# Self-attention value products in four row groups of 32 by 128 columns, their weights turned on VectorE, tokens laid in halves of four sequences

## What is computed

```
x = x + tanh(g_xattn) * xattn(layernorm(x), ctx)         # 16 heads of 128, 64 keys, q and k rms-normed
y = layernorm(x)
q, k, v = rmsnorm(y)*ln1 @ wq, wk, wv                    # self-attention, 16 heads of 128
attn = softmax(causal(q k^T / sqrt(128)))                # 64 x 64 for each sequence and head
y = y + (attn v) @ wo
t = rmsnorm(y)*ln2
routed = top-6 of 16 experts (176 units each), weighted; shared = one expert of 352 units
x = x + tanh(g_ffn) * (y + routed + shared)
```

## Time and profile before

| | |
|---|---|
| median of 3 runs | 628.91 us (628.39 to 629.61) |
| the profiled execution | 628.85 us |
| its span, first to last instruction | 627.1 us |
| PE, PEld | 619.1 us (99%), 541.5 us (86%) |
| DVE, ACT, POOL | 462.0 us (74%), 320.5 us (51%), 253.3 us (40%) |
| granted TensorE clock | 1.000 over the whole span |

### The profile page before, as it was taken

The page is one execution under the profiler, slowest core; times in us unless marked ns, Lnnn a source line. Parts: engine busy times, 40 slices in busy tenths (PEclk is TensorE's granted clock), DMA queues, the critical chain, the costliest instruction groups (busy, mean ns, idle before and its releaser), DMA issues.

```text
span 627.1 us, 18234 instructions
## 1 busy us (share of the span) xinstructions
PE 619.1 (99%) x7200; PEld 541.5 (86%) x7200; DVE 462.0 (74%) x930; ACT 320.5 (51%) x699; POOL 253.3 (40%) x336
## 2 busy tenths in 40 slices
PE   8999999999999999999999999999999999999997
PEld 6788888888889988999999889988888888888886
DVE  5979777997886886786677899565576987555556
ACT  6867677777743334242434333453477444444442
POOL 3221211313144334344343354345545665455453
PEclk9999999999999999999999999999999999999999
DMA  7532131111021322222231321123323233333332
GB/s 234 186 85 70 52 103 28 40 40 31 24 70 43 111 69 69 70 68 77 64 118 39 115 70 36 35 63 93 98 85 94 75 102 101 90 87 99 100 87 90
DMA packets 36023, 50.30 MB, mean 80 GB/s; under 512 B 4080, under 2 KB 23024, under 8 KB 35952
## 3 DMA queue, kind: packets, MB, share of 16 engines
q1 hardware_dynamic: 35376, 48.81, 26.2%
q10 hardware_dynamic: 576, 0.48, 0.2%
HBM read 48.22 MB, written 1.05 MB: 79 GB/s over the span
## 4 chain that ended last, share of the span: by engine, by line
PE 96%; DVE 1%; ACT 1%; DMA 1%; issue 1%; SPq 0%; DVEq 0%; ACTq 0%
PE acc L568 26%; PE bank_q L541 17%; PE bank_k L541 14%; PE bank_v L541 9%; PE bank_s L541 8%; PE bank_v L656 7%; PE bank_k L736 2%; PE bank_p L753 2%; PE bank_s L714 2%; PE bank_s L704 2%; PE bank_t L721 1%; PE bank_p L687 1%; PE bank_q L677 1%; PE bank_k L666 1%; DMA xt<-in_ctx_t 1%
## 5 line engine op out<-in xcount | busy, mean ns | idle before, releaser
L568 PE MATMUL acc<-wo_hi,pv_hi 128*128 128x256 f32 x328 | 93.4, 285 | 0.4 <-DVE pv_lo L1515 0.2
L568 PE MATMUL acc<-wo_lo,pv_hi 128*128 128x256 f32 x328 | 92.9, 283 | 0.0
L568 PE MATMUL acc<-wo_hi,pv_lo 128*128 128x256 f32 x328 | 92.0, 281 | 0.0
L1677 POOL TENSOR_TENSOR wq_lo<-raw_a,wq_hi 128x256 fp32r<-128x256 f32 x32 | 23.4, 732 | 116.9 <-DVE wq_hi L1452 116.9
L568 PEld LDWEIGHTS acc<-wo_hi,pv_hi 128*128 128x128 f32 x328 | 61.5, 188 | 5.3 <-issue 2.2
L1677 POOL TENSOR_TENSOR wq_lo<-raw_m,wq_hi 128x256 fp32r<-128x256 f32 x50 | 40.4, 808 | 59.8 <-DVE wq_hi L1471 58.3
L568 PEld LDWEIGHTS acc<-wo_lo,pv_hi 128*128 128x128 f32 x328 | 61.6, 188 | 2.2
L568 PEld LDWEIGHTS acc<-wo_hi,pv_lo 128*128 128x128 f32 x328 | 62.3, 190 | 0.0
L1515 DVE TENSOR_TENSOR pv_lo<-raw_a,pv_hi 128x512 fp32r<-128x512 f32 (+1 forms) x51 | 37.5, 737 | 31.8 <-ACT pv_hi L1104 31.5
L1104 ACT ACTIVATE pv_hi<-raw_a 128x512 fp32r<-128x512 f32 (+1 forms) x51 | 31.7, 623 | 56.1 <-DVE raw_a L1510 50.5
L541 PE MATMUL bank_q<-xt_hi,wq_hi 128*128 128x512 f32 x144 | 59.8, 415 | 0.0
(11 more groups left out here) (246 smaller groups left out, 1949.2 us busy)
## 6 DMA issues: line engine op xcount, KB each, us to landing
raw_m<-in_chunk_m SPq DMA_DIRECT2D x50, 256.0 KB, 2.8
raw_a<-in_head_a SPq DMA_DIRECT2D x48, 192.0 KB, 3.3
raw_b<-in_head_b SPq DMA_DIRECT2D x32, 256.0 KB, 3.0
raw_m<-in_chunk_m SPq DMA_DIRECT2D x50, 128.0 KB, 2.1
raw_v<-in_pair_v SPq DMA_DIRECT2D x16, 256.0 KB, 2.8
raw_b<-in_head_b SPq DMA_DIRECT2D x32, 128.0 KB, 2.1
xs<-in_x SPq DMA_DIRECT2D x6, 128.0 KB, 3.2
out<-xs SPq DMA_DIRECT2D x3, 256.0 KB, 2.5
```

Source lines behind the costliest of these rows:

```text
L568: last = nc.tensor.matmul(acc[t // 2][:, (t % 2) * D:(t % 2 + 1) * D], w[:, tok], m, start=begins and n == 0, stop=True, skip_group_check= ...
L1677: nc.gpsimd.tensor_tensor(lo, raw, hi, ALU.subtract).then_inc(signal, 1)
```

## The change

**Tokens.** The host lays `x` out so that a tile of 128 tokens holds one half (32 tokens) of each of four sequences. Tile `2n + part` has half `part` of sequences `4n` to `4n+3`. Before, it held two whole sequences. The output is laid back on the host. Access patterns change with it (`tokens_of`, `keys_of`, `queries_at`).

**Turning.** `turn_attn` on TensorE and `take_turned` on ScalarE go. `turn_weights` on VectorE (blocks of 32 by 32) now serves self-attention too.

**Value products.** They are formed in four row groups `j` of 32 rows by all 128 columns, each into its own bank, `bank_k`, `bank_v` (in the last pair `bank_q`), `bank_p`, `bank_t`. `k` runs over the two halves of the keys. For the first half (`k == 0`) both halves of the queries move (64 columns), for the second only the later one (32 columns), since the mask leaves the others at nothing. They leave PSUM in four steps instead of two.

**Around it.** `bank_k` and `bank_v` are now written by the value products, so the keys of the next pair's first head go to `bank_s`, and `head_values` waits until ScalarE has taken the values out of `bank_v`. Rounding `wo` moves from VectorE (`split_out`, L1485) to ScalarE (`round_out`). VectorE's `split_head_values` moves ahead of `subtract_max`. In cross-attention `place_variance` (L812, 8 small matmuls at the start of each half) goes, since the statistics now lie where they are added. In stage `m`, `bank_s` and `bank_k` change places.

```diff
         def turn_banks(u):
-            return (bank_t, bank_p) if u.kind == "a" else (bank_p, bank_s if u.kind == "b" else bank_t)
+            return (bank_t, bank_p) if u.kind == "a" else (bank_p, bank_t)
...
+        def head_bank(u, j):
+
+            return (bank_k, bank_v if u.deferred else bank_q, bank_p, bank_t)[j]
...
         def key_bank(u, h):
...
-            return (bank_s, bank_q)[h] if u.very_first else bank_k
+            return (bank_s, bank_q if u.very_first else bank_k)[h]
...
-            def turn_attn(u):
-                pe.wait_ge(B["norm"], u.n)
-                for b in range(G // 2):
-                    last = nc.tensor.transpose(bank_t[:, b * P:(b + 1) * P],
-                                               attn[:, 2 * b:2 * b + 2, :].rearrange("p t k -> p (t k)"), ident)
-                last.then_inc(B["t_done"], 1)
...
             def head_values(u):
 
                 pe.wait_ge(B["vs"], 2 * u.n)
                 pe.wait_ge(B["attn_t"], u.n)
-                turned = rows_t[:].rearrange("p n a q -> p (n a q)").rearrange("p (n a h q) -> p n h a q", a=2, h=2, q=GROUP)
+                if u.deferred:
+                    pe.wait_ge(B["vs"], 2 * u.n + 2)
+                else:
+                    pe.wait_ge(M["silu"], 1)
+                turned = rows_t[:].rearrange("p t h q -> p (t h q)")\
+                    .rearrange("p (a h n k q) -> p h n k a q", a=2, h=2, n=2, q=GROUP)
                 values = vs[u.n % 2]
-                for g in range(G):
-                    h, n = divmod(g, NT)
-                    cols = slice(g * SEQ, (g + 1) * SEQ)
-                    for c in range(P // SEQ):
-                        width = slice(h * P + c * SEQ, h * P + (c + 1) * SEQ)
-                        for r in range(SPB):
-                            rows = slice(r * SEQ, (r + 1) * SEQ)
-                            last = nc.tensor.matmul(value_bank(r)[c * SEQ:(c + 1) * SEQ, cols], values[rows, n, width],
-                                                    turned[rows, n, h], start=True, stop=True)
+                for h in range(2):
+                    for n in range(2):
+                        for k in range(2):
+                            for j in range(QUADS):
+                                rows = slice(j * GROUP, (j + 1) * GROUP)
+                                found = by_token(head_bank(u, j))[:, h, 2 * n + k:2 * n + 2]
+                                last = nc.tensor.matmul(found, values[rows, 2 * n + k, h * P:(h + 1) * P],
+                                                        turned[rows, h, n, k, k:], start=k == 0, stop=True,
+                                                        skip_group_check=True)
                 last.then_inc(B["pv_done"], 1)
...
             def take_head_values(u):
                 act_e.wait_ge(B["pv_done"], u.n)
-                for r in range(SPB):
-                    nc.scalar.activation(by_sequence(pv_hi[:], r), by_tile(value_bank(r)[:]), ACT.Copy).then_inc(B["pv_hi"], 1)
+                for j in range(QUADS):
+                    nc.scalar.activation(tokens_of(pv_hi[:], j), by_token(head_bank(u, j)), ACT.Copy).then_inc(B["pv_hi"], 1)
+
+            def round_out(u, h):
+                if u.n > 1:
+                    act_e.wait_ge(B["wo_done"], u.of(h) - 2)
+                act_e.wait_ge(ld_b2[h], 16 * u.n)
+                nc.scalar.activation(wo_hi[h][:], raw_b2[h][:], ACT.Copy).then_inc(B["wo_hi"], 1)
```

More of the change, by code:

```diff
@@ L413, in up_bank @@
         def up_bank(u):
-            return (bank_k, bank_s)[u.parity]
+            return (bank_s, bank_k)[u.parity]
         x_v = x.rearrange("(h t p) d -> h p t d", h=HALVES, p=P)
@@ L581, in output @@
                 else:
-                    pe.wait_ge(B["pv_lo"], u.of(1))
+                    pe.wait_ge(B["pv_lo"], QUADS * u.n)
                     pe.wait_ge(B["wo_lo"], u.of(h))
@@ L630, in project_keys @@
                 pe.wait_ge(stage["wk_lo"], u.of(h))
-                if h and bank is bank_k and u.kind == "b":
-                    pe.wait_ge(B["kt"], u.of(0))
+                if not h and u.kind == "b" and not u.very_first:
+                    pe.wait_ge(B["scaled"], u.n - 1)
                 if h and bank is bank_q:
@@ L702, in scores @@
                             at = (n * QUADS + j) * SEQ
-                            queries = slice(at + part * GROUP, at + (part + 1) * GROUP)
                             last = nc.tensor.matmul(bank_s[j * GROUP:(j + 1) * GROUP, g * SEQ:(g + 1) * SEQ],
-                                                    qt[:, h, queries], kt[:, h, at:at + SEQ], start=True, stop=True)
+                                                    qt[:, h, queries_at(n, part, j)], kt[:, h, at:at + SEQ], start=True, stop=True)
                     last.then_inc(A["scores"], 1)
@@ L711, in scores @@
                     for j in range(QUADS):
-                        at = (2 * j + n) * SEQ
-                        queries = slice(at + part * GROUP, at + (part + 1) * GROUP)
-                        last = nc.tensor.matmul(bank_s[j * GROUP:(j + 1) * GROUP, g * SEQ:g * SEQ + seen], qt[:, h, queries],
-                                                kt[:, h, at:at + seen], start=True, stop=True)
+                        keys = kt[:, h].rearrange("p (n a j c) -> p n j a c", a=2, j=QUADS, c=GROUP)[:, n, j, 0:part + 1]
+                        last = nc.tensor.matmul(bank_s[j * GROUP:(j + 1) * GROUP, g * SEQ:g * SEQ + seen],
+                                                qt[:, h, queries_at(n, part, j)], keys, start=True, stop=True)
                 last.then_inc(B["scores"], 1)
-            def turn_attn(u):
-                pe.wait_ge(B["norm"], u.n)
-                for b in range(G // 2):
-                    last = nc.tensor.transpose(bank_t[:, b * P:(b + 1) * P],
-                                               attn[:, 2 * b:2 * b + 2, :].rearrange("p t k -> p (t k)"), ident)
-                last.then_inc(B["t_done"], 1)
             def context_values(u):
@@ L767, in prepare @@
                 piece, step = piece_at(u)
-                if piece in ("turn", "logits", "spread") and u.kind == "b":
-                    pe.wait_ge(B["scaled"], u.n)
                 if piece == "turn":
@@ L803, in release @@
                     pe.wait_ge(semaphore, value)
-            def place_variance(u):
-                pe.wait_ge(eps_ready, u.half + 1)
-                variance = eps_var[:, u.half, :].rearrange("p (n t) -> p t n", n=2)
-                for j in range(QUADS):
-                    for part in range(2):
-                        row = j % 2 * SEQ + part * GROUP
-                        nc.tensor.matmul(bank_q[j * GROUP:(j + 1) * GROUP, HT // 2 + part * 2:HT // 2 + part * 2 + 2],
-                                         ident[:, row:row + GROUP], variance[:, j // 2], start=True, stop=True)
             def cross_pair(u):
@@ L869, in self_pair @@
                     project_gate(nxt)
+                    pe.wait_ge(B["scaled"], u.n)
                     project_up(nxt)
-                    pe.wait_ge(B["pv_lo"], prev.of(1))
+                    pe.wait_ge(B["pv_lo"], QUADS * prev.n)
                     prepare(u)
@@ L876, in self_pair @@
                     held = prepare(u)
-                turn_attn(u)
                 if nxt.kind == "b":
@@ L893, in chunk @@
                 if u.very_first:
+                    pe.wait_ge(B["pv_lo"], QUADS * (prev.n - 1) + 1)
                     project_up(nxt, range(1))
@@ L1153, in self_pair @@
                         split_up(after, nxt.of(0))
+                if nxt.kind == "m":
+                    gate(nxt)
                 prepare(u)
-                take_turned(u)
                 prepare(u, 1)
+                for h in range(2):
+                    round_out(u, h)
                 if nxt.kind == "b":
@@ L1604, in self_pair @@
                     split_keys(after, 0, nxt)
-                for h in range(2):
-                    split_out(u, h)
                 if not early:
@@ L1838 @@
     r = run_bass_kernel_spmd(nc, [{f"in_{n}": laid[n] for n in _INS}], core_ids=[0])
-    return r.results[0]["out"].reshape(inputs["x"].shape)
+    found, shape = r.results[0]["out"], inputs["x"].shape
+    return found.reshape(-1, 2, 4, SEQ // 2, shape[-1]).transpose(0, 2, 1, 3, 4).reshape(shape)
```

78 lines of the change are left out of this document (34 added, 44 removed).

## The result

The changed kernel takes 638.14 us (median of 4 runs, 637.39 to 639.07), the kernel before 629.26 beside it (628.39 to 629.70). The ratio is 1.0144, with an interval of 1.0125 to 1.0163: slower by 1.4%. The forecast was 634.6 in a range of 632.5 to 639.0. The result lies in the range, but 3.5 us above the forecast, and most of what follows is about these 3.5 us.

A forecast was written before the change was run, and what follows sets the result against it. TensorE's stream was taken as the bound. Value products +0.83 and transposes -0.45, times 16, gave +6.1 us; less 0.3 for statistics, +5.8 on 628.85 made 634.6 us, range 632.5 to 639.0.

The forecast's parts named there:

- The load sets the step: Value products: 128-column weight loads set steps of about 0.112 us, 1.92 us against 1.09, +0.83 a pair.
- Rival 1: Value products: matmuls, not loads, set the step; products cost 0.88 us, total 618.0 us; chance 0.12.
- rival 3: Value products: one of a matmul's two loads hides; window about 1.46 us, total 627.3 us; chance 0.04.
- The logits with 16 moving columns: Router logits, loading 32 columns and moving 16: 36 ns a step, taken as evidence that the step follows the load.
- The reservation on them: Router logits: four issues of 8 to 9 ns might equally explain the 36 ns step.
- The transposes: Between outputs and queries: removing L721 saves 0.36 us and the return from plain fp32 0.09, together 0.45 a pair.
- the variance: Start of both halves: removing L812 saves 0.15 us each, together 0.3.
- Rival 2: Loads set the step, plus a new wait for ScalarE's `bank_v` copy or splits: +3 us, 637.6; chance 0.18.
- the two roundings: ScalarE gains two rounds of `wo` from VectorE; both engines had over 4 us free in a pair.
- The gap: Pair after the plain one: 0.50 us lost, unexplained by the program; one such gap left in the sum.

The follow-up runs named there:

- e1_narrow: Changed kernel, but every value product moves only 32 columns, leaving out late queries' products with early keys; 637.20 us, ratio 1.0139.
- e2_wide: Changed kernel, but every value product moves 64 columns, the second key half's too; 639.02 us, ratio 1.0158.
- e11_grouped: Changed kernel with second-key-half products in 32x64 tiles after all 32x128 ones, `wo` roundings behind the first-values copy; doesn't compute the layer; 639.61 us, ratio 1.0159.
- e7_shift: Changed kernel with 4 of 16 warm-up matmuls replaced by 64 small ones, shifting later instructions by 120; 636.91 us, ratio 1.0114.
- e9_both: Changed kernel with `wo` roundings behind the copy freeing `bank_v`, and 64 small and 12 large warm-up matmuls; 636.70 us, ratio 1.0109.
- e10_shift256: Changed kernel with 132 small and 12 large warm-up matmuls, shifting later instructions by 256; 638.85 us in one run.
- e4_turns: Changed kernel with four unused plain fp32 identity transposes put back between outputs and queries in 15 pairs; 641.85 us, ratio 1.0201.
- e5_round: Changed kernel with ScalarE's roundings of `wo` moved behind the copy that frees `bank_v`; 636.94 us, ratio 1.0110.
- the repeat: The changed kernel run again without any edit, beside the runs on moved columns; 638.41 us, ratio 1.0142.
- e3_half64: Changed kernel with each value product cut into two tiles of 32x64, 128 loads and 128 matmuls a pair; 663.26 us, ratio 1.0535.

## Why the prediction was right, and where its sizes were off

**The load sets the step: right.** Predicted were loads of 187 ns, steps of 0.11 at both widths, and 1.92 us. All three came in as forecast, and e1_narrow and e2_wide show that it is the load. Rival 1 falls with them, and rival 3 too, which would have had steps of 0.11 and 0.056 in turn and products of some 1.5 us. (The text says 1.46; with the ends of the earlier trace rows its own terms give 1.53.) The logits with 16 moving columns pointed the right way. The reservation on them, that four issues may cost as much as their 36 ns, was fair, and it stays open: the 16 narrow rounds of e11_grouped, with four loads and four matmuls each, start 0.03 us apart at their quickest and 0.04 on average. What decides is e1_narrow and e2_wide, not the logits. The outputs had the time that was forecast, too: the last `pv_lo` was ready 1.96 us after the projection behind the products began (1.99 forecast).

**The transposes: right by themselves, but most pairs kept 0.08 that was not in the sum.** I took off 0.45 a pair, 0.36 for L721 and 0.09 for the return from plain fp32 to fp32r. The queries did fall from 1.47 to 1.39. But in most pairs the values and keys behind them rose, from 4.24 in all to 4.31 (254.65 to 258.96). So a plain pair is 0.47 longer, which is 14.25, and not 0.38. Over 16 pairs that is 7.5, less 0.3 for the variance 7.2, where I had 5.8. This is 1.4 of the 3.5 us. It isn't a fixed price of taking the transposes out: the pairs of 14.16 in e7_shift, e9_both and e10_shift256 have the same instructions and are as long as the forecast said, and e4_turns stands 0.44 above them. What slows the later projections by 0.08 in one pair and not in the next, no run here tells.

**The waits: the kind was named, the place was not.** Rival 2 had ScalarE late with `bank_v`. I looked at a plain pair, where 0.17 us were left, and cost it at nothing, and there it held. The wait came in the one pair whose ScalarE queue also holds the squares at a late point, and at the copy before the second value projection, not at `head_values`. Its cost is 0.7 in the view of waits and 0.87 in the length of the pair (15.12 against 14.25). I had listed the two roundings that move to ScalarE as free, because the engine is busy for half of a pair. The free time was there, but not in front of that copy. The roundings are 0.56 of the 0.87, as e5_round shows. The rest comes from the products and the transposes: the squares begin 0.83 later in the pair, and the transposes, which gave ScalarE time before the projections, are gone (with them back, in e4_turns, the wait is 0.3). In the last stage, the split that TensorE waits for costs 0.6 in place of 0.2. It is 0.6 in all runs with the change, and I made no run for it.

**The gap: left in the sum at its old size.** I carried over one gap of 0.50, since nothing in the program explained it. The profiled execution had 1.85 (16.10 less 14.25), the repeat 3.26, of which about half is the lower clock level behind the wait. The runs showed that it is a wait for instructions, and that the dense stretch of scores and value products is where it falls. The step that failed is to treat an unexplained gap as a constant while changing the stretch it lies in.

**The sum of the profiled execution**: 7.2 for the pairs, 1.85 - 0.50 = 1.35 for the gap, 0.87 and 0.4 for the two waits make 9.8, measured are 9.6. The sign and the main term were right for the right reason. That the result still fell into the range is in part luck: its upper end of 639.0 was there for rival 2, and two thirds of the 3.5 us come from the gap and from pairs that kept 0.08, which the range had not been made for.

## What to carry to other kernels

When tiles run side by side with few moving columns, price a step by the columns that are loaded, not by those that move. A split into more rows and fewer banks only pays if the loaded width does not grow. Look at the queue of a helping engine in the one pair that differs from the others, not only in a plain one: free time on an engine is worth something only if it lies ahead of what is waited for. And count instructions in a dense stretch: halving the tiles won 0.43 us a pair on the array, and lost 2 us a pair in waits for instructions and in stretches at the lower clock level behind them.

## What the runs showed of the hardware beyond that

- A stretch of many short loads and matmuls can run TensorE out of instructions. Instruction packets of 16 KB take 0.9 to 2.0 us, and the engine goes on 2.2 to 2.8 us after the packet's start (twice 3.4). The waits came to 0.2 us in the kernel before, 1.5 and 1.6 in the two profiles of the changed one and 19.8 in e3_half64. A small shift of the instructions (e7_shift, e10_shift256) removed the one of the changed kernel.
- Such a wait can be followed by a stretch at the lower clock level, 1.2 GHz: there was none behind 1.6 us in the changed kernel, one stretch behind 1.5 in the repeat, and 27 us in six stretches in e3_half64. A query and a key projection, 2.87 us together, take 5.29 in it.
- A change between 32x128 and 32x64 tiles costs about 0.13 us (0.16 to 0.22 from start to start).
- Four loads and four matmuls in 32x64 tiles can be through in 0.03 us (e11_grouped, 261.85 to 261.88). Of the seven steps between the first eight such rounds six take 0.03 us, the later ones 0.05 on average.
